# Two-layer graph network: every 80th and every 128th tile of edges fetched row by row from SyncE

## What is computed

```python
h = relu(layernorm(x))
x = x + segment_sum((h @ W.T + b)[src] * edge_weight[:, None], dst)
h = relu(layernorm(x))
m = concat([h[src], h[dst]])                 # 106,250 x 256
msg = sum over types t of where(edge_type == t, relu(m @ W1[t] + b1[t]) @ W2[t] + b2[t], 0)
agg = segment_sum(msg, dst)
x = x + GRU(agg, h)                          # sigmoid gates r, z, tanh candidate, 128 wide
```

## Time and profile before

| what | us |
|---|---|
| time, median of 3 runs | 2150.04 (2149.90 to 2151.04) |
| the profiled execution's own time | 2151.11 |
| its span, first to last instruction | 2149.4 |
| POOL busy | 1585.1 |
| PE busy | 1275.7 |
| DVE busy | 900.7 |
| ACT busy | 569.6 |

### The profile page before, as it was taken

The page is one execution under the profiler, slowest core; times in us unless marked ns, Lnnn a source line. Parts: engine busy times, 40 slices in busy tenths (PEclk is TensorE's granted clock), DMA queues, the critical chain, the costliest instruction groups (busy, mean ns, idle before and its releaser), DMA issues.

```text
span 2149.4 us, 23739 instructions
## 1 busy us (share of the span) xinstructions
PE 1275.7 (59%) x6652; PEld 1084.8 (50%) x6652; DVE 900.7 (42%) x2535; ACT 569.6 (27%) x1502; POOL 1585.1 (74%) x1677
## 2 busy tenths in 40 slices
PE   2445445445455455454556677677777776776775
PEld 2434334334344343343346666666666666666665
DVE  7732233233233233233234555545545545545554
ACT  4623333333333323333231111111111111111111
POOL 6777777777777777777567777777777777777774
PEclk7566666566666666566677987888888798888888
DMA  8323223223233223223244444444444444444442
GB/s 181 94 79 98 78 79 99 77 79 99 77 80 99 77 79 98 77 79 99 59 127 112 105 115 110 112 111 112 113 112 109 113 116 106 114 116 108 115 112 54
DMA packets 176204, 213.84 MB, mean 99 GB/s; under 512 B 53644, under 2 KB 121962, under 8 KB 175569
## 3 DMA queue, kind: packets, MB, share of 16 engines
q0 software_dynamic: 53248, 109.16, 21.2%
q1 hardware_dynamic: 121577, 102.33, 16.4%
q10 hardware_dynamic: 1244, 0.79, 0.2%
HBM read 176.56 MB, written 35.56 MB: 99 GB/s over the span
## 4 chain that ended last, share of the span: by engine, by line
POOL 73%; issue 24%; PE 1%; DMA 1%; DVE 1%; ACT 0%; POOLq 0%; SPq 0%; DVEq 0%; ACTq 0%
POOL accs L1248 36%; POOL G L1581 15%; POOL edge L1581 15%; POOL g_more L1581 7%; DMA accs<-in_edge_weight_dram 0%; PE bank L1522 0%; DMA accs<-h_tab,src_t 0%; PE bank L1485 0%; DMA edge<-p_tab,src_t 0%; DMA p_tab<-hot 0%; PE bank L1785 0%; PE bank L1762 0%; ACT accs L1402 0%; PE bank L1775 0%; PE bank L1786 0%
## 5 line engine op out<-in xcount | busy, mean ns | idle before, releaser
L1248 POOL DMA_INDIRECT accs<-h_tab,src_t x776 | 732.7, 944 | 236.5 <-issue 236.2
L1752 PE MATMUL bank<-qwin,hotT 128*128 128x128 f32 x1664 | 292.4, 330 | 313.8 <-DVE hotT L1646 302.6
L1485 PE MATMUL bank<-accs 128*125 128x133 f32 x1664 | 334.4, 372 | 227.1 <-ACT accs L1402 177.1
L1485 PEld LDWEIGHTS bank<-accs 128*125 128x125 f32 x1664 | 312.0, 274 | 270.8 <-issue 132.2
L1752 PEld LDWEIGHTS bank<-qwin,hotT 128*128 128x128 f32 x1664 | 246.8, 228 | 352.7 <-DVE hotT L1646 340.6
L1581 POOL DMA_INDIRECT G<-p_tab,src_t x336 | 320.0, 952 | 126.3 <-issue 103.0
L1581 POOL DMA_INDIRECT edge<-p_tab,src_t x336 | 318.9, 949 | 102.4 <-issue 102.4
L1402 ACT ACTIVATE accs<-accs,edge 128x128 f32<-128x128 f32 x776 | 247.6, 391 | 492.7 <-DMA accs<-h_tab,src_t 491.9
L1710 ACT ACTIVATE rows<-rows 128x512 f32<-128x512 f32 x208 | 130.9, 629 | 673.2 <-DVE rows L1654 673.2
L1762 PE MATMUL bank<-hot,rows 128*128 128x128 f32 x1664 | 285.9, 329 | 5.8 <-ACT rows L1710 5.2
L1762 PEld LDWEIGHTS bank<-hot,rows 128*128 128x128 f32 x1664 | 268.9, 245 | 6.2 <-ACT rows L1710 6.2
(11 more groups left out here) (175 smaller groups left out, 1332.0 us busy)
## 6 DMA issues: line engine op xcount, KB each, us to landing
qwin<-q_tab SPq DMA_DIRECT2D x416, 64.0 KB
nodew<-key_tab SPq DMA_DIRECT2D x52, 256.0 KB
nodehot<-key_tab SPq DMA_DIRECT2D x52, 256.0 KB, 3.6
accs<-h_tab,src_t POOLq DMA_INDIRECT x776, 2.6
p_tab<-st SPq DMA_DIRECT2D x25, 224.0 KB
p_tab<-hot SPq DMA_DIRECT2D x25, 224.0 KB
q_tab<-st SPq DMA_DIRECT2D x25, 224.0 KB
q_tab<-hot SPq DMA_DIRECT2D x25, 224.0 KB
```

The costliest lines, as they stand in the source:

```text
L1248: eng.indirect_dma_start(slot0(o % R0)[:, t, 0:D], None, x if o < EARLY else h0_tab, bass.IndirectOffsetOnAxis(src_t[:, k:k + 1], 0)).then ...
L1485: ins = eng.matmul(pb[SUM_BANK[o % 4]][0:CW, 0:FW], ones_of(o % HR)[:, t, :], slot0(o % R0)[:, t, :], start=t == 0, stop=t == TO - 1)
L1752: ins = eng.matmul(pb[2 + g % 2][:, t * D:(t + 1) * D], hotT[:, g % HT, t * P:(t + 1) * P], qwin[:, g % NG, t // PR, :], start=True, stop= ...
```

## The change

Some tiles are no longer gathered by POOL. SP fetches their rows one by one, each with a transfer of its own whose source address comes out of a register: in layer 0 tile 7 of the octets 18, 28, ... 98 (nine tiles) and tile 830 (10 rows), in layer 1 tile 3 of the groups 36, 68, ... 196 (six tiles) and tile 830. The rows of a tile are spread over ten octets (12 or 13 an octet), or 32 groups (4 a group); the last row of a tile is issued three octets, or three groups, before the octet or group that needs it. Each tile's row numbers are read beforehand into one partition of SBUF, and 32 of them are loaded into registers at a time. The rows land in one of two buffers (a third of `hotT` in layer 0, half of `w1a` in layer 1, both unused there), and ACT (layer 0) or DVE (layer 1) reads that buffer in place of the slot. Tile 831, which is empty, is left out everywhere. For layer 1, ACT converts the row numbers of `p_tab` to integers once, and SP stores them. `f0_sp` now runs by the step counter, pair work first, then rows. `bases` loads eight registers for four groups in `f1_sp`.

```diff
+        BATCH = 32
+        ALONE0 = [((6 + 10 * j + 12) * TO + TO - 1, [(6 + 10 * j + i, P * i // 10, P * (i + 1) // 10) for i in range(10)]) for j in range(9)]
+        ALONE0.append((NTILE - 1, [(97, 0, E - (NTILE - 1) * P)]))
+        ALONE1 = [((2 + 32 * j + 34) * GT + GT - 1, [(2 + 32 * j + i, P * i // 32, P * (i + 1) // 32) for i in range(32)]) for j in range(6)]
+        ALONE1.append((NTILE - 1, [(202, 0, E - (NTILE - 1) * P)]))
...
+        def sp_row_numbers(eng):
+            eng.wait_ge(s["row_no"], 1)
+            eng.dma_start(row_tab.rearrange("(p e) -> p e", p=PB), typ_i.rearrange("p g e -> p (g e)")).then_inc(s["row_st"], 16)
+
+        def row_values(eng, numbers, a, b, top):
+            _, v = nc.values_load_multi_w_load_instructions(
+                numbers[0:1, a:b], engines=[eng.engine], min_val=0, max_val=top,
...
+        def act_row_numbers(eng):
+            eng.wait_ge(s["keys_in"], 1)
+            eng.activation(typ_i, src4_a, ACT.Copy).then_inc(s["row_no"], 1)
...
                 for t in range(TO):
                     k = o * TO + t
+                    if k in alone0 or k >= NTILE:
+                        continue
                     eng.indirect_dma_start(slot0(o % R0)[:, t, 0:D], None, x if o < EARLY else h0_tab,
...
-                        ins = eng.activation(G0[:, t, 0:D], G0[:, t, 0:D], ACT.Copy, scale=w_t[:, o * TO + t:o * TO + t + 1])
+                        k, row = o * TO + t, G0[:, t, 0:D]
+                        if k >= NTILE:
+                            continue
+                        if k in alone0:
+                            j = alone0[k]
+                            eng.wait_ge(s_a0[j % 2], rows_alone(ALONE0, j))
+                            row = row_alone0(j)
+                        ins = eng.activation(G0[:, t, 0:D], row, ACT.Copy, scale=w_t[:, o * TO + t:o * TO + t + 1])
...
+            def rows_by_number(j, a, b):
+                if a == 0:
+                    numbers(j + 1)
+                    eng.wait_ge(s_no0[j % 2], 16 * (j // 2 + 1))
+                    if j >= 2:
+                        eng.wait_ge(s["dv0"], 2 * (ALONE0[j - 2][0] // TO) + 2)
+                for r in range(a, b):
+                    if r % BATCH == 0:
+                        held[:] = row_values(eng, rows_no0, j % 2 * P + r, j % 2 * P + min(r + BATCH, ALONE0[j][1][-1][2]), N - 1)
+                    eng.dma_start(row_alone0(j)[r:r + 1, :], h0_tab[bass.ds(held[r % BATCH], 1), :]).then_inc(s_a0[j % 2], 16)
+
+            held = []
+            numbers(0)
+            eng.wait_ge(s["tab"], 32 * len(T_PIECES))
+            for o in range(STEPS0 + 1):
+                if (p := pair_at(o, 1)) is not None:
+                    p_rows_out(p)
+                if (p := pair_at(o, 2)) is not None:
+                    q_rows_out(p)
+                if o in issue0:
+                    rows_by_number(*issue0[o])
...
-                    if g % 2 == 0:
-                        base = bases(eng, (g + 2) * GP, 2 * GP)
+                    if (g + 2) % NG == 0:
+                        base = bases(eng, (g + 2) * GP, NG * GP)
...
+                if g in issue1:
+                    rows_by_number(*issue1[g])
...
-                eng.tensor_tensor(rows[:, g % 2], pb[2 + g % 2][:, :].rearrange("p (t d) -> p t d", d=D), slot1(g % R1),
-                                  ALU.add).then_inc(s["sum1"], 1)
+                got = pb[2 + g % 2][:, :].rearrange("p (t d) -> p t d", d=D)
+                n = next((t for t in range(GT) if g * GT + t in alone1), GT)
+                ins = eng.tensor_tensor(rows[:, g % 2, 0:n], got[:, 0:n], slot1(g % R1)[:, 0:n], ALU.add)
+                if n < GT:
+                    j = alone1[g * GT + n]
+                    eng.wait_ge(s_a1[j % 2], rows_alone(ALONE1, j))
+                    ins = eng.tensor_tensor(rows[:, g % 2, n], got[:, n], row_alone1(j), ALU.add)
+                ins.then_inc(s["sum1"], 1)
```

More of the change, by code:

```diff
@@ L207, in gnn_program, with row_alone0, row_alone1, rows_alone @@
         EARLY = 7
+        BATCH = 32
[3 more added lines that the diff above has]
+        ALONE1.append((NTILE - 1, [(202, 0, E - (NTILE - 1) * P)]))
+        alone0, alone1 = ({k: j for j, (k, _) in enumerate(a)} for a in (ALONE0, ALONE1))
+        issue0, issue1 = ({o: (j, a, b) for j, (_, part_s) in enumerate(al) for o, a, b in part_s} for al in (ALONE0, ALONE1))
+        assert NTILE == NT - 1 and NTILE % GT == 3
+        def row_alone0(j):
+            return hotT[:, 2, j % 2 * D:(j % 2 + 1) * D]
+        def row_alone1(j):
+            return w1a[:, j % 2, :]
+        rows_no0 = hotT[0:1, 0, P:3 * P].bitcast(I32)
+        rows_no1 = w1b[0:1, 0:2, :].rearrange("p a d -> p (a d)").bitcast(I32)
+        def rows_alone(al, j):
+            return 16 * sum(b - a for _, part_s in al[j % 2:j + 1:2] for _, a, b in part_s)
+        def gathered0(o, h):
+            return 16 * sum(o_ * TO + t not in alone0 and o_ * TO + t < NTILE
+                            for o_ in range(o % R0, o + 1, R0) for t in range(h * GT, (h + 1) * GT))
+        def gathered1(g):
+            return 16 * sum(g_ * GT + t not in alone1 and g_ * GT + t < NTILE for g_ in range(g % R1, g + 1, R1) for t in range(GT))
         key16 = accs[0:PB, K16:K16 + ECOL // 2].bitcast(BF16)
@@ L269, in gnn_program @@
         s_xl = [sem(f"s_xrows{q}") for q in range(2)]
+        s_a0 = [sem(f"s_alone0_{q}") for q in range(2)]
+        s_a1 = [sem(f"s_alone1_{q}") for q in range(2)]
+        s_no0 = [sem(f"s_number0_{q}") for q in range(2)]
+        s_no1 = [sem(f"s_number1_{q}") for q in range(2)]
         s_k = [sem(f"s_keys{q}") for q in range(2)]
@@ L368, in sp_keys @@
             eng.dma_start(key_tab.rearrange("(p e) -> p e", p=PB), key16).then_inc(s["key_st"], 16)
+        def sp_row_numbers(eng):
[4 more added lines that the diff above has]
+                numbers[0:1, a:b], engines=[eng.engine], min_val=0, max_val=top,
+                skip_runtime_bounds_check_because="they are row numbers of the graph's edges, as the gathers read them")
+            return v
         def sp_x(eng):
@@ L1481, in octet @@
                     eng.wait_ge(s["acc0"], o - 3)
-                for t in range(TO):
+                last = min(TO, NTILE - o * TO) - 1
+                for t in range(last + 1):
                     if t % GT == 0:
@@ L1485, in octet @@
                     ins = eng.matmul(pb[SUM_BANK[o % 4]][0:CW, 0:FW], ones_of(o % HR)[:, t, :], slot0(o % R0)[:, t, :],
-                                     start=t == 0, stop=t == TO - 1)
+                                     start=t == 0, stop=t == last)
                 ins.then_inc(s["out0"], 1)
@@ L1551, in f0_sp, with p_rows_out @@
                     eng.dma_start(h0_lin[h, a:b, :], t_rows[i][h]).then_inc(s["tab"], 16)
-            for p in range(NPAIR):
+            def p_rows_out(p):
                 if p + 2 < NPAIR:
@@ L1568, in f0_sp, with numbers @@
                 eng.dma_start(c_rows[:, 2 * p:2 * p + 2, :], cntb[0:T, :, :]).then_inc(s["st_c"], 16)
+            def numbers(j):
+                if j < len(ALONE0):
+                    k = ALONE0[j][0]
+                    n = min(P, E - k * P)
+                    eng.dma_start(rows_no0[:, j % 2 * P:j % 2 * P + n], src[k * P:k * P + n].rearrange("(a e) -> a e", a=1)
+                                  ).then_inc(s_no0[j % 2], 16)
+            def rows_by_number(j, a, b):
[18 more added lines that the diff above has]
+                    rows_by_number(*issue0[o])
         PQ_STORED = 16 + 32 * NCH
@@ L1580, in f1_pool @@
                     k = g * GT + t
+                    if k in alone1 or k >= NTILE:
+                        continue
                     eng.indirect_dma_start(slot1(g % R1)[:, t, :], None, p_rows,
@@ L1750, in expand @@
                     eng.wait_ge(s["sum1"], g - 1)
-                for t in range(GT):
+                for t in range(min(GT, NTILE - g * GT)):
                     ins = eng.matmul(pb[2 + g % 2][:, t * D:(t + 1) * D], hotT[:, g % HT, t * P:(t + 1) * P],
@@ L1759, in sums @@
                     eng.wait_ge(s["acc1"], (g - 1) * GP)
-                for t in range(GT):
+                last = min(GT, NTILE - g * GT) - 1
+                for t in range(last + 1):
                     p = t // PR
                     ins = eng.matmul(pb[4 + g % 2][:, p * KEYS:(p + 1) * KEYS], rows[:, g % 2, t, :], hot[:, g % NG, t, :],
-                                     start=t % PR == 0, stop=t % PR == PR - 1)
+                                     start=t % PR == 0, stop=t % PR == PR - 1 or t == last)
                 ins.then_inc(s["out1"], 1)
```

35 lines of the change are left out of this document (28 added, 7 removed).

## The result

The changed kernel takes 2121.99 us in the median of four runs (2121.62 to 2123.71), the kernel before 2150.31 us in the runs beside it (2149.90 to 2151.04): a ratio of 0.9869, 95% interval 0.9852 to 0.9887. The gain is 28.3 us, where 25.0 were forecast; 2122.0 lies inside the range of 2120 to 2133. The gain showed on the chip of this comparison and, with variants of the changed kernel, on one of the three on which the experiments ran. On the other two, met by chance, the kernel before itself takes 2551 and 2582 us; there the changed kernel (on one of them) and its 15 full tiles alone (on both) cost 7%. So this part has two results to explain.

A forecast was written before the change was run, and what follows sets the result against it. POOL's gather queue was taken as the bound (97% of the chain). Gathers removed, 13.7 us in layer 0 and 10.0 in layer 1, plus ends of 0.85 and 0.4, sum to 25.0 us: 2125.0 us, range 2120 to 2133.

The forecast's parts named there:

- the bound: Whole kernel: POOL's queue of gathers and the short pauses between them make 97% of the chain that ended last.
- the cover: SP's added work fits beside POOL's gathers: 87 of 99.9 us per ten octets, 17.7 of 20.1 us per four groups.
- the main terms: Gathers removed from POOL: layer 0 11 x 1.249 = 13.7 us, layer 1 8 x 1.256 = 10.0 us.
- Layer 1: Eight gathers fewer in layer 1 (six full tiles, 830 and 831) at 1.256 us each save 10.0 us.
- they may vanish or double: Odd long gathers of layer 1, 5.8 us above layer 0's pitch, a term that can move inside the forecast.
- The ends: Less last work for ACT, PE and DVE shortens the end of layer 0 by 0.85 us, layer 1 by 0.4 us.
- A row at 0.53 us: SP's price per single-row transfer with its register instructions, taken from a window; 0.43 at best, 0.73 at worst.
- The load of 32: SP's register load of 32 row numbers takes 2.1 us; ends of the range 0.6 and 7.3 us.
- Rival A: SP can't keep up in layer 0 at 0.73 us a row, so POOL waits: 2219 us; chance 0.05.
- B: SP's transfers slow POOL's gathers by 15 ns each, 29 us for 1940: 2154 us, gain gone; chance 0.04.
- D: SP's loads of 32 cost 0.23 us a register, four make 29.2 us instead of 8.4: 2175 us; chance 0.02.
- C: Rows come late in single places, an SP stall beyond its lead costs 20 to 25 us: 2145 to 2150; chance 0.04.

The follow-up runs named there:

- spread: Kernel before, padded lanes of tiles 830 and 831 given 128 different row numbers instead of row 0: 2550.56 us, ratio 0.9997; repeated on another chip 2581.30 us, 1.0001.
- rows_twice: Changed kernel with every single row of layer 0 fetched twice by SP, ACT waiting for all: 2235.01 us, ratio 1.0382 to the kernel before.
- full_only: Changed kernel with SP fetching only the 15 full tiles, POOL gathering 830 and 831: 2739.15 us, ratio 1.0735; repeated on another chip 2765.39 us, 1.0717.
- no_rows: Changed kernel without the 1940 single-row transfers, register loads kept, a tile of ones in their place: 2122.43 us, ratio 0.9861 to the kernel before.
- after_2: Changed kernel itself, unedited, on a chip where the kernel before took 2581.56 us: 2763.84 us, ratio 1.0715.
- every56_88: Changed kernel with SP fetching every 56th tile of layer 0 (13) and every 88th of layer 1 (9): 3084.15 us, ratio 1.1952 to the kernel before.
- rows_half_again: Changed kernel with every second single row of layer 0 fetched a second time, 192 transfers a tile: 2119.66 us, ratio 0.9843 to the kernel before.

## Why the prediction was right, and where not

The time came out inside the range because the bound, the price of a gather and the cover were right. It did so on a chip where SP ran at full pace; that such a chip was met is luck, which the forecast did not provide for. On the other kind it would have been wrong by its sign.

**The bound and the main terms** were right. 11 gathers fewer in layer 0 gave 13.83 us for 13.7, at an unchanged pitch of 1.249.

**Layer 1** gave 11.96 for 10.0. The other 2 us are in the term that the prediction kept as "they may vanish or double". The second gather of the layer started 0.92 us late before (1084.03 us after 1081.86) and on time after (1067.78 after 1066.53). That isn't chance: it is late in all three profiles of the kernel before and `spread`, and on time in all eleven of the changed kernel and its variants; why stays open. The odd long gathers add up to 4.0 us over the median instead of 5.2; this part varies (2.6 to 4.3 in three other profiles of changed kernels), and here it was luck.

**The ends** were undersized: 0.85 and 0.4 us forecast, 2.59 and 1.75 found. The step that failed read the earlier trace rows for ACT, PE and DVE alone and passed over the column behind them, the wait for the gather, although 3.88 and 4.15 us could be worked out from the earlier trace rows. Tile 831 wasn't just one more gather: it was the slowest to land, and the last. That is 1.33 and 1.54 us of the 3.1 missing here; what shares of ACT and PE were forecast (0.85 and 0.4) leave 0.2 unexplained.

**A row at 0.53 us** was too dear; it is 0.41, below the lower end of 0.43. The window, which I took as nearest, is addressed in the same way, but its transfer instruction is dearer (342 ns, a row's is 228); the single row with a fixed address (244 ns) was the nearer one. Nothing hung on that in the sum, since the work was covered either way. **The load of 32** at 2.1 us was right; the trace has 2120 ns, 66 ns a register. The estimate of 6.4 us, worked out from the 200 ns a register of the Trainium skill's "Runtime: NRT & Kernel Launch", section "Instruction fetch mechanics", does not hold for these loads out of SBUF.

**Rival A** was right as a mechanism, 20 us too cheap (`rows_twice`), and wrong as a chance. I judged it by what a row costs at its worst (0.73 us, from the slowest load of x rows). It came true on two of the three chips of the experiments (in the changed kernel on one, in `full_only` on both), through something the price of an instruction doesn't show, the pace of the whole sequencer. Nothing in the profile of the kernel before could have told of it: SP's longest MOVE there is 37 ns in the windows' line. **B** is refuted by `no_rows`, **D** by the 2120 ns. **C** did not happen on the first kind of chip; 28 us to spare in 99.9, not 13, kept it away.

## What to carry to other kernels

An idle sequencer can take over single-row fetches from a bound gather queue at 0.41 us a row. At 92% of its budget in layer 0 they cost nothing; at 113% the whole excess was paid, lead or no lead. Such a trade turns slack into a bound, so keep a margin for the sequencer's pace and not only for its prices, and time it on more than one chip: here the same kernel took 1.3% less on one and 7.2% more on another. Look at which gather stands last, and at the delay until its first user: padded lanes that all point at one row made it land 1.3 to 1.6 us later. Different row numbers cost nothing on the two chips where they ran; what they bring where POOL is the bound was not timed.

## What the runs showed of the hardware

- In the kernel before, a gather whose lanes read one row 118 to 128 times takes 257 to 383 ns a packet instead of 130, and its last packet ends 3.4 to 4.0 us after its start instead of 2.2 to 2.3.
- 1940 register-addressed transfers of 512 bytes beside POOL's gathers slow them by nothing measurable (`no_rows` 2122.43 us, the changed kernel 2121.99, `rows_half_again` with 2521 transfers 2119.66).
- On two of the three chips of the experiments the kernel before takes 19 and 20% longer than the 2150 us shown. On them SP's instructions of every kind pause for about 0.70 us at a time, with the medians of the row instructions unchanged, and SP does 51 to 59% of the work per time in layer 0 that it did on the first chip (`after_2`, `every56_88`).
